# Two seams of a transformer layer: the gated block's first norm moved into the local attention's last units, and the local stage's first rows and weights moved into the stage ahead of it

## The reference

```python
sa, ca, ga, sb, cb, gb = ...                       # from silu(L1_c) @ L1_wmod
h = _layernorm(x) * (1 + ca) + sa
x = x + ga * _L1_attn_ref(h, Wq, Wk, Wv, Wo)       # windowed attention
h = _layernorm(x) * (1 + cb) + sb
x = x + gb * _L1_ffn_ref(h, ...)                   # the local stack:

def _layer(x, ...):                                # DEPTH = 2
    h = shift_token(x)                             # second half of a row from the row before
    q, k, v = split(h @ wqkv)
    q = l2norm(q) * qs;  k = l2norm(k) * ksc
    q, k = rotary_xpos(q, k)
    o = local_attention(q, k, v)                   # windows of 128, each with the one before
    x = x + o @ wo
    h = shift_token(x)
    h = (h - mean) / sqrt(var + 1e-05) * lg + lb
    a, g = split(h @ w1 + b1)
    return x + (a * gelu(g)) @ w2 + b2
```

## Time and profile before

| | us |
|---|---|
| median of 3 runs | 3439.26 (3437.61 to 3439.87) |
| the profiled execution | 3436.8 |
| its span, first to last instruction | 3435.1 |
| PE busy | 3159.2 (92%) |
| DVE busy | 1936.2 (56%) |
| ACT busy | 1575.8 (46%) |
| GpSimd busy | 724.3 (21%) |
| mean granted PE clock | 0.958 of full |

### The profile page before, as it was taken

The page is one execution under the profiler, slowest core; times in us unless marked ns, Lnnn a source line. Parts: engine busy times, 40 slices in busy tenths (PEclk is TensorE's granted clock), DMA queues, the critical chain, the costliest instruction groups (busy, mean ns, idle before and its releaser), DMA issues. The chain is left out here.

```text
span 3435.1 us, 46202 instructions
## 1 busy us (share of the span) xinstructions
PE 3159.2 (92%) x15128; PEld 1817.9 (53%) x15129; DVE 1936.2 (56%) x4725; ACT 1575.8 (46%) x3537; POOL 724.3 (21%) x861
## 2 busy tenths in 40 slices
PE   8899998977999969999987999997998999997998
PEld 4455555544666623333324666664555666665555
DVE  6999994541111126666645878773223777775322
ACT  5666652211222226666654666662222656564221
POOL 0000003560000045555532322220001111110111
PEclk9999998998999969999998999998999999998999
DMA  4000004012111111111002000000001000000000
GB/s 145 1 1 1 1 0 167 28 58 92 45 45 44 43 41 28 28 32 30 22 15 65 10 9 10 10 5 27 0 0 34 9 10 8 10 6 4 13 13 25
DMA packets 81274, 97.37 MB, mean 28 GB/s; under 512 B 14611, under 2 KB 68263, under 8 KB 80811
## 3 DMA queue, kind: packets, MB, share of 16 engines
q1 hardware_dynamic: 74106, 76.65, 6.9%
q0 software_dynamic: 6960, 18.10, 1.7%
HBM read 60.35 MB, written 24.13 MB: 25 GB/s over the span
## 5 line engine op out<-in xcount | busy, mean ns | idle before, releaser
L2302 PE MATMUL ps_loc_psa<-sb_stk_w,sb_loc_hT 128*128 128x512 f32 x768 | 350.1, 606 | 5.3 <-DMA sb_stk_wo<-in_loc_wo 3.6
L1706 DVE CUSTOM_DVE_ANT_0 sb_win_masked<-ps_win_pss,sb_win_around 128x384 f32<-128x384 f32 (+1 forms) x512 | 256.3, 538 | 175.0 <-PE ps_win_pss L1801 174.8
L2589 PE MATMUL ps_mlp_ps<-sb_mlp_hT,sb_stk_w 128*128 128x512 f32 (+1 forms) x768 | 322.5, 613 | 22.2 <-DVE sb_mlp_hid L2542 22.2
L2099 ACT ACTIVATE sb_loc_pr<-ps_loc_psw,sb_loc_nb,sb_loc_sc 128x256 f32<-128x256 f32 x512 | 281.0, 569 | 114.4 <-DVE sb_loc_nb L2227 114.4
L1801 PE MATMUL ps_win_pss<-sb_win_kT,sb_win_q 32*128 32x384 f32 (+1 forms) x1024 | 235.2, 531 | 38.1 <-DVE sb_win_qtok L1706 35.7
L1612 ACT ACTIVATE sb_win_pT<-ps_win_pst 128x512 f32<-128x512 f32 x368 | 199.8, 595 | 124.4 <-PE ps_win_pst L1812 122.3
L2542 DVE SCALAR_TENSOR_TENSOR sb_mlp_hid<-ps_mlp_ps,sb_stk_col,sb_mlp_gl 128x512 f32<-128x512 f32 x96 | 71.7, 749 | 303.3 <-ACT sb_mlp_gl L2511 303.3
L2511 ACT ACTIVATE sb_mlp_gl<-ps_mlp_ps,sb_stk_col 128x512 f32<-128x512 f32 x96 | 65.9, 687 | 381.7 <-PE ps_mlp_ps L2589 381.5
L2302 PEld LDWEIGHTS ps_loc_psa<-sb_stk_w,sb_loc_hT 128*128 128x128 f32 x768 | 142.1, 192 | 181.6 <-issue 177.7
L2589 PEld LDWEIGHTS ps_mlp_ps<-sb_mlp_hT,sb_stk_w 128*128 128x128 f32 (+1 forms) x768 | 130.3, 184 | 201.4 <-issue 201.4
L709 PE MATMUL ps_rec_psp<-sb_rec_hT,sb_rec_w 128*128 128x512 f32 x512 | 235.4, 604 | 0.8 <-DVE sb_keep_modf L466 0.8
(11 more groups left out here) (313 smaller groups left out, 6468.1 us busy)
## 6 DMA issues: line engine op xcount, KB each, us to landing
sb_exp_rows<-sorted_tokens SPq DMA_DIRECT2D x72, 128.0 KB, 2.0
expert_results<-sb_exp_res SPq DMA_DIRECT2D x72, 128.0 KB, 1.7
sb_moe_w_in<-in_L_ffn_w_in_eDF SPq DMA_DIRECT2D x8, 512.0 KB, 11.3
sb_moe_w_sw<-in_L_ffn_w_swiglu_eDF SPq DMA_DIRECT2D x8, 512.0 KB, 11.4
sb_exp_w_out<-in_L_ffn_w_out_eFD SPq DMA_DIRECT2D x8, 512.0 KB, 7.1
sb_win_sums<-sb_win_raw SPq DMA_DIRECT2D x128, 32.0 KB, 2.0
sb_stk_angles<-in_angles SPq DMA_DIRECT2D x32, 128.0 KB, 3.8
out_y<-sb_stk_y SPq DMA_DIRECT2D x8, 512.0 KB, 2.9
```

Of the source, the lines that this page charges most:

```text
L1706: nc.vector.tensor_tensor_reduce(masked[:, pair % 2, j, 0:keys], pss[:, (n + j) % PLAIN, 0:keys], around[:, first:first + keys], 1.0, -3e3 ...
L2099: e = nc.scalar.activation(pr[:, hf, h], psw[:, hf, h // 2, h % 2 * 256:h % 2 * 256 + 256], ACT.Exp, scale=sc8[:, b, hh:hh + 1], bias=nb[: ...
L2302: t = nc.tensor.matmul(psa[:, c], hT[:, b, k, 1 - k:P + 1 - k], w[:, k, c * 512:(c + 1) * 512], start=(k == 0), stop=(k == KD - 1))
L2589: i = nc.tensor.matmul(ps[at:at + M, q % 2, i2], w1[:, k, i2 * HID + f * P:i2 * HID + f * P + M], hT[:, b, k], start=(k == 0), stop=(k == ...
```

## The change

Seam one, windowed into local attention. The loads of the local stage's attention weights, its first four angle tiles (SP) and its masks (GpSimd, at the end of its list) are issued in the windowed stage. Its first three input rows (LEAD = 3: tiles 0, 16 and 1) are normalised and modulated there too, into a buffer of their own, `lead`: statistics at slot 5 and offsets at slot 7 of step 32 on DVE, deviation at slot 6 of step 32 and scaling at slot 2 of step 33 on ACT, modulation at the end of GpSimd's list. The local stage reads these rows through `rows_in`. The windowed stage has seven more semaphores to be cleared.

Seam two, local attention into the gated block, in both layers. The gated block's norm buffers for b = 0 live longer, and the norm of its block 0 is made in the local stage: statistics of b = 0 at the end of unit 28 and of b = 1 at the end of unit 29 (`statistics_of`), inverse deviation of both behind `copy_sums(30)`, scaling of b = 0 at the end of unit 30, its turns into free PSUM banks in unit 31 between scores and turns, the affine step at the end of ACT's list. The shift of the last tile is issued at the start of the gated block, and the local stage no longer waits for shifts at its end. In the gated block `up(0)` is PE's first work; DVE scales b = 1 once the shifts have landed, PE turns it after `up(1)`, ACT finishes it after gelu(1). To make room, `riT` is gone: `copy_sums` writes oT, which `scale_output` then scales in place. Two rows that only the experts need are freed earlier, and the gates are numbered anew.

The diff, cut to its core:

```diff
+LEAD = 3
+FIRST_UNITS = NB * 4
...
+    def hold(self, m, b):
+
+        self.xn[b] = m.sb(f"xn{b}", [P, TB, D])
+        self.hT[b] = m.sb(f"hT{b}", [P, KD, BLK])
...
+    def statistics_of(self, dve, it, b, j):
+        nc = self.nc
+        for t in range(TB):
+            parts = self.halves(b, t, j)
+            for k, part in enumerate(parts):
+                i = nc.vector.bn_stats(self.stats[:, b, t, k], part)
+        i.then_inc(self.s_st, 1)
+        dve.wait_ge(self.s_st, it * NB + b + 1)
+        for t in range(TB):
+            i = nc.vector.bn_aggr(self.mv[:, b, t], self.stats[:, b, t, 0:len(self.halves(b, t, j))])
+        i.then_inc(self.s_mv, 1)
...
+                load_attention_weights(sp, a, S, 0)
+                for j in range(RING):
+                    sp.dma_start(S["angles"][:, j], a["angles"][:, j]).then_inc(S["loc"][f"angles_in{j}"], 16)
...
+                for dst, name in ((S["mask"], "loc_mask"), (S["identb"], "ident")):
+                    pool.dma_start(dst[:], a[name]).then_inc(S["loc"]["masks_in"], 16)
+                for i in range(LEAD):
+                    b = i % NB
+                    pool.wait_ge(s_lxn, i + 1)
+                    nc.gpsimd.tensor_tensor(lead[:, i], lead[:, i], keep["scale_row"][:, b], ALU.mult).then_inc(s_lym, 1)
+                    pool.wait_ge(s_lym, i + 1)
+                    nc.gpsimd.tensor_tensor(lead[:, i], lead[:, i], keep["shift_row"][:, b], ALU.add
+                                            ).then_inc(S["loc"]["in"], 1)
...
+                        if k == 6 and s == NT:
+                            lead_deviation()
+                        if k == 2 and s == NT + 1:
+                            lead_rows()
+
+                def lead_deviation():
+                    act.wait_ge(s_lmv, 1)
+                    nc.scalar.activation(lead_lnv[:], lead_mv[:, :, 1], ACT.Ln, bias=keep["eps"][:, 0:1]).then_inc(s_lln, 1)
+                    act.wait_ge(s_lln, 1)
+                    nc.scalar.activation(lead_rstd[:], lead_lnv[:], ACT.Exp, scale=-0.5).then_inc(s_lrstd, 1)
+
+                def lead_rows():
+                    act.wait_ge(s_lnmr, 1)
+                    for i in range(LEAD):
+                        nc.scalar.activation(lead[:, i], x[:, lead_tile(i)], ACT.Identity, scale=lead_rstd[:, i:i + 1],
+                                             bias=lead_nmr[:, i:i + 1]).then_inc(s_lxn, 1)
...
+                        if k == 5 and s == NT:
+                            lead_statistics()
+                        if k == 7 and s == NT:
+                            lead_offsets()
+
+                def lead_statistics():
+                    dve.wait_ge(s_x, max(lead_tile(i) for i in range(LEAD)) + 1)
+                    for i in range(LEAD):
+                        last = nc.vector.bn_stats(lead_stats[:, i], x[:, lead_tile(i)])
+                    last.then_inc(s_lst, 1)
+                    dve.wait_ge(s_lst, 1)
+                    for i in range(LEAD):
+                        last = nc.vector.bn_aggr(lead_mv[:, i], lead_stats[:, i])
+                    last.then_inc(s_lmv, 1)
+
+                def lead_offsets():
+                    dve.wait_ge(s_lmv, 1)
+                    dve.wait_ge(s_lrstd, 1)
+                    nc.vector.scalar_tensor_tensor(out=lead_nmr[:], in0=lead_mv[:, :, 0], scalar=-1.0, in1=lead_rstd[:],
+                                                   op0=ALU.mult, op1=ALU.mult).then_inc(s_lnmr, 1)
...
+        def rows_in(i):
+
+            return S["lead"][:, i] if L == 0 and i < LEAD else y[:, at(i)[2]]
...
-                if L == 0:
-                    load_attention_weights(sp, a, S, 0)
-                for j in range(RING):
-                    load_angles(j)
+                if L:
+                    for j in range(RING):
+                        load_angles(j)
                 load_mlp_weights(sp, a, S, L)
-                for i in range(TILES):
+                for i in range(TILES - 1):
                     j, b, tile = at(i)
                     sp.wait_ge(s_y, F + i + 1 + L + 1)
-                    src = y[:, tile, P:D]
-                    sp.dma_start(xs_b[1:P, b, j], src[0:P - 1]).then_inc(s_xs, 16)
-                    sp.dma_start(xs_b[0:1, b, j + 1], src[P - 1:P]).then_inc(s_xs, 16)
+                    src, done = y[:, tile, P:D], s_xs0 if i < FIRST_UNITS else s_xs
+                    sp.dma_start(xs_b[1:P, b, j], src[0:P - 1]).then_inc(done, 16)
+                    sp.dma_start(xs_b[0:1, b, j + 1], src[P - 1:P]).then_inc(done, 16)
                     if b and j + RING < TPB:
                         load_angles(j + RING)
-                sp.wait_ge(s_xs, (L + 1) * TILES * 32)
...
-                if L == 0:
-                    modulate(0)
-                    modulate(1)
                 pool.wait_ge(s_k8, (L + 1) * 16)
                 tables(0)
-                if L == 0:
-                    modulate(2)
...
-                    nc.scalar.copy(riT[:], psw[:, 0, 0]).then_inc(s_riT, 1)
+                    nc.scalar.copy(oT[:], psw[:, 0, 0]).then_inc(s_riT, 1)
...
+                    if i == TILES - 2:
+                        norm.inverse_deviation(act, I0)
+                    if i == TILES - 1:
+                        act.wait_ge(S["mlp"]["w_in"], (L + 1) * 80)
+                        for k in range(KD):
+                            norm.affine_chunk(act, I0, 0, k, psa[:, k])
...
+                    if i == TILES - 4:
+                        dve.wait_ge(s_y, F + FIRST_UNITS + L + 1)
+                        dve.wait_ge(s_xs0, (L + 1) * FIRST_UNITS * 32)
+                        norm.statistics_of(dve, I0, 0, 0)
+                    if i == TILES - 3:
+                        norm.statistics_of(dve, I0, 1, 0)
+                    if i == TILES - 2:
+                        norm.scale_rows(dve, I0, 0, 0)
...
+                    if i == TILES - 1:
+                        for k in range(KD):
+                            norm.turn(pe, I0, 0, k, psa[:, k], first=True)
...
+                tail = y[:, NB * TPB - 1, P:D]
+                sp.dma_start(xs_b[1:P, NB - 1, TPB - 1], tail[0:P - 1]).then_inc(s_xs, 16)
+                sp.dma_start(xs_b[0:1, NB - 1, TPB], tail[P - 1:P]).then_inc(s_xs, 16)
...
-                deviation(I0)
-
                 act.wait_ge(s_w, (L + 1) * 80)
-                for b in range(NB):
-                    affine(I0, b)
...
+                        if j == 0 and q == 1:
+                            affine(I0, 1)
...
-                norm.statistics(dve, I0, 0)
-
                 dve.wait_ge(s_w, (L + 1) * 80)
-                for b in range(NB):
-                    norm.scale_rows(dve, I0, b, 0)
-
+                dve.wait_ge(s_xs, (L + 1) * (TPB * NB - FIRST_UNITS) * 32)
+                norm.scale_rows(dve, I0, 1, 0)
...
-                turn(I0, 0, first=True)
+                        norm.turn(pe, it, b, k, pst[:, k])
 
                 pe.wait_ge(s_w, (L + 1) * 80)
-
-                pe.wait_ge(norm.s_hT, norm.ready(I0, 0))
-                turn(I0, 1, first=True)
...
+                        if j == 0 and q == 1:
+                            turn(I0, 1)
```

206 lines of the change are left out of this document (111 added, 95 removed).

## The result

| | kernel before | changed kernel |
|---|---|---|
| median of the runs, us | 3439.57 (3437.61 to 3440.13, 4 runs) | 3407.22 (3404.22 to 3408.84, 4 runs) |
| profiled execution, us (span) | 3436.8 (3435.1) | 3408.32 (3406.6) |

The ratio is 0.9906 with a 95% interval of 0.9889 to 0.9923, so 32.4 us less on the medians, where 32.9 were forecast; 3406 was predicted and 3407.2 measured. The interval means 26 to 38 us less, so an agreement within 1 us is finer than the measurement. The two profiled spans differ by 28.5 us only.

A forecast was written before the change was run, and what follows sets the result against it. PE is busy 99.92 of 100 us inside a local stage, leaving the seams between stages: 6.1 us into the local stage plus 26.8 at two gated-block seams, 32.9 off 3436.8, plus 2.5 to the median, gives 3406; range 3402 to 3411.

The forecast's parts named there:

- Seam into the gated block: Local attention into gated block, twice: up(2) starts 8.8 us after the last addition, in place of 25.2; 16.4 us gained.
- late tail of a rival: Gated block, layer 0: shifted tile lands later behind 2 MB of weights; with low clock 3 us per seam, 3412; chance 0.14.
- low clock at the block's start: Gated block's first 6 us at low clock, 2.4 us late per seam; with late tail 3 us, 3412; chance 0.14.
- last unit's gap grew as foretold: Sign of being right: PE's gap in the local stage's last unit grows to some 4.5 us less the turns.
- Statistics in units 28 and 29: Local stage: 2.05 us of vector-engine work per unit costs 0.7 us each, 1.4 together; GpSimd's spread chain has no slack.
- Scaling ahead of the last maxima: Local stage's last unit: 2.25 us of scaling for b = 0, less 0.65 idle, costs 1.6 us, all of it counting.
- rival by which more is gained: Last units: statistics fit into pauses and turns keep the clock up, 1.4 + 1 us per seam, 3401.5; chance 0.08.
- Seam into the local stage: Windowed into local attention, layer 0: first scores 15.76 us after the start, not 22.80; 7.0 us gained, 6.1 net.
- clearing: Between windowed and local stage: seven more semaphore-clearing instructions cost 0.4 us.
- tail: Windowed stage's end: ACT's logarithm and exponential for three rows, ahead of invert_sums(30), cost 0.5 us.
- The windowed stage's start: Seven more transfers share DMA engines with the gathers: cost 0, bounds 0 and 2.5 us; rival that the stage pays 0.09.
- GpSimd idle before its first addition: Sign of being wrong, at the windowed stage's start: GpSimd waits for a gather, where roughly 2 us of cover was taken.

The follow-up runs named there:

- spread_stats: Changed kernel with the gated block's sixteen first-row statistics made two to a unit in units 20 to 27; median 3442.1 us, 0.9910 of the kernel before.
- late_loads: Changed kernel with the seven early transfers moved behind SP's wait for the six memsets; median 3443.3 us, 0.9914 of the kernel before.
- tail_wait: Changed kernel with the gated block's vector-engine wait for the last shifted tile moved behind the rows of b = 1; median 3440.2 us, 0.9905 of the kernel before.
- no_loads: Changed kernel with three rows made ahead, but weights, angles and masks loaded by the local stage itself; median 3448.7 us, 0.9925 of the kernel before.

## Why the prediction was right, point by point

**The total.** 3406 forecast, 3407.2 measured. Both halves' mechanisms were right. Sizes that were off cancel: the seams into the gated blocks gave 28.1 in place of 26.8, the seam into the local stage is worth some 4 after its costs in place of 6.1. That the total agrees within 1 us, with an interval of 6 us either way, is luck; that it lies near 33 us is not.

**Seam into the gated block.** The pause of 12.7 us became 0.9; up(2) came 8.8 us behind the last addition in layer 1, as forecast, and 9.6 in layer 0. The 0.8 us more is the transfer of the last tile: the vector engine had it 6.0 us after SP issued it (5.1 forecast, 5.2 in layer 1), with the next layer's weights issued right behind it and the DMA engines full in layer 0 only. That is the late tail of a rival, at about a quarter of its price; that the weights cause it is likely and was not tested. The low clock at the block's start, the other half of that rival, did not come: 1.00 in every window of the first ups. The last unit's gap grew as foretold, 0.83 + 1.09 (the turns) + 2.57 = 4.5 us. The whole block, from the last addition to its end, became 15.3 and 15.5 us shorter in the two layers (16.4 forecast), and each local stage, from first scores to last addition, 1.4 us longer (3.0 forecast): a smaller gain and a smaller cost, which cancel.

**Statistics in units 28 and 29.** 0.7 each forecast, 0.47 measured, and PE's wait of 0.26 us for GpSimd's spread lies on the chain that was named. spread_stats shows the bound: 0.4 us a unit, and 0.7 for the aggregates, are free.

**Scaling ahead of the last maxima.** This step was mis-sized. 1.6 us forecast; the maxima were late by 1.5, as worked out, but the unit became only 0.1 and 0.3 us longer, because the stretch at the lower clock was 3.4 us long and not 6.8. With 6.8 us, as in late_loads and spread_stats, the unit took 16.7 to 17.5, so 1.4 to 2.2 more than in the kernel before, where 1.6 was forecast. The shorter stretch was half of the rival by which more is gained, which laid it to the turns of b = 0 in the gap; in which way they do it no run shows. It is not certain in each execution: in late_loads, tail_wait, no_loads and spread_stats one or both last units took 16.7 to 17.5.

**Seam into the local stage.** 15.76 us to the first scores forecast, 15.66 measured; clearing 0.4 forecast, 0.5 measured; tail 0.5 forecast, 0.22 measured.

**The windowed stage's start.** This is the step that failed, and its sign (GpSimd idle before its first addition) was on the prediction's list. I took 0 for the gathers with 2.5 as the bound; GpSimd waited 2.20 to 2.83 us in all eight profiles with the early transfers and never in the six without. The cover of 2 us was read from the median landing of 2.8; the gather itself landed after 3.3, so it was 1.5. The larger error was to leave the landing where it was: it became 7.1 us, about the 7.3 of the upper bound (the early loads themselves took 9.8 to 10.7). The Trainium skill ("DMA: Bandwidth & Descriptors", section "Queues, rings and completion order") has an engine take turns between queue rows, a packet at a time. I made of it that a gather waits for one packet at most and so for 1 us, which that section does not say; the gather landed 3.8 us later, and the measurement decides against that reading. By the view of the DMA queues four gathers are 192 packets in the trace, which makes three for each engine and gather if they are spread evenly, and each may wait its turn, so the rule as it stands does not contradict the 7.1 us; whether that is what happened, no run here shows.

**What no step had.** The granted clock in the windowed stage adds or spares 1.6 us a unit for two to four units, whatever the kernel. In the pair of profiles that is two units, 3.2 us, of the some 4 us that the first seam is worth. In the gated block of layer 0 it does the same: behind one pause of 3.7 us, sixteen matmuls took 7.11 us in seven of the fourteen profiles, 8.80 in four and 9.66 in three.

## What to carry to other kernels

Before a transfer is moved to an earlier stage, look at what that stage's first instructions gather, and price the move at the landing time under load, not at the idle one. Where two chains end at one point, moving only the one that does not end last gains nothing, and in the one profile here it was even 1.6 us slower. A gain or a loss of 1 to 6 us between two profiles of a kernel with many short pauses of PE is not yet the change's: look for units with the same waits and another granted clock, and profile the kernel before again.

## What was not expected of the hardware

- The same pause of 0.62 us of PE is followed by some 3 us at the lower clock in two to four units of the windowed stage and by none in the others, in two profiles of one and the same kernel too, which are from two chips; each costs 1.6 us.
- Behind a pause of 2.6 to 3 us the clock was at its lower level for 3.4 or 6.8 us or not at all, in layers of one and the same execution, which makes the last unit of one kernel 13.9 or 14.4 us long, of another 15.4 or 17.3. With twenty transposes without use in that pause it stayed at 1.00 in both layers.
- In the gated block of layer 0, behind the same pause of 3.7 us, the clock fell for 0, 3.4 or 6.8 us, and sixteen matmuls took 7.11, 8.80 or 9.66 us.
- After a pause of 0.93 to 1.03 us between two stages it stayed at 1.00 in all twenty-four seams seen with the change; behind the pause of 12.7 us of the kernel before it was at the lower level for 7.7 of the ten us behind the last addition.
- With 2.6 MB of loads issued beside it, the second gather of the windowed stage landed after 7.1 us in place of 3.3.
